# First FFN stage: two gate tiles of a chunk ahead of the next chunk's transposes, and the first chunk rounded and transposed tile by tile

## The reference, cut to what matters

```
x = layernorm(x)                       # 4096 rows of 256
x = act_qdq(x)                         # one scale for the whole tensor: max|x| / 32767, rounded to int16 steps
up   = act_qdq(x @ dequant(w_up).T)    # 256 -> 768
gate = act_qdq(x @ dequant(w_gate).T)  # 256 -> 768, again one scale for the whole tensor
gate = act_qdq(gate * fixed_qdq_u16(sigmoid(gate)))
o    = act_qdq(gate * up)
return o @ dequant(w_down).T
```

## Time and profile before

| | us |
|---|---|
| median of 3 runs | 1246.44 |
| lowest and highest of the 3 | 1245.01, 1251.27 |
| the profiled execution, its own time | 1250.26 |
| its span, first to last instruction | 1248.5 |
| TensorE matmuls busy | 1074.1 (86%) |
| VectorE busy | 954.4 (76%) |
| ScalarE busy | 620.5 (50%) |
| GpSimd busy | 428.0 (34%) |
| mean granted TensorE clock | 0.934 of full speed |

### The profile page before, as it was taken

One profiled execution on the slowest core, in us unless ns is written; L12 is line 12 of the kernel. 1 busy time (PEld: TensorE's weight loads), 2 busy tenths in 40 slices (PEclk: granted clock), 3 DMA queues, 4 the chain that ended last, 5 costly groups with the idle time before them and its releaser, 6 DMA issues. The chain is left out here.

```text
span 1248.5 us, 21557 instructions
## 1 busy us (share of the span) xinstructions
PE 1074.1 (86%) x6208; PEld 897.2 (72%) x6208; DVE 954.4 (76%) x2586; ACT 620.5 (50%) x1332; POOL 428.0 (34%) x514
## 2 busy tenths in 40 slices
PE   7899999995998981039977599999999969999998
PEld 5677777874886760039944588888898858788786
DVE  4798998874675998976554677788878758888886
ACT  1667766761565996977445233333333322333333
POOL 1344444440001882000011235544554443334333
PEclk9999999995998995559999799999999988999999
DMA  8000000000233765702213500101000000000000
GB/s 264 1 2 2 1 1 1 2 1 29 107 120 122 265 252 197 236 22 64 68 43 106 174 1 1 42 0 42 0 0 0 1 1 9 25 18 17 25 17 26
DMA packets 35551, 71.87 MB, mean 58 GB/s; under 512 B 3531, under 2 KB 23071, under 8 KB 35295
## 3 DMA queue, kind: packets, MB, share of 16 engines
q1 hardware_dynamic: 34111, 70.28, 16.9%
q10 hardware_dynamic: 1376, 0.79, 0.3%
HBM read 40.41 MB, written 30.65 MB: 57 GB/s over the span
## 5 line engine op out<-in xcount | busy, mean ns | idle before, releaser
L1068 PE MATMUL a_ps<-VW,a_PT 128*128 (+1 forms) x640 | 143.7, 379 | 0.0
L1068 PEld LDWEIGHTS a_ps<-VW,a_PT 128*128 128x128 f32 x640 | 119.3, 190 | 15.2
L1106 ACT ACTIVATE a_U<-a_U 128x1280 f32<-128x1280 f32 x32 | 40.6, 1270 | 112.6 <-DVE a_U L1179 112.6
L1085 ACT COPY a_PT<-a_ps 128x512 f32<-128x512 f32 (+1 forms) x96 | 46.1, 518 | 90.2 <-PE a_ps L1031 90.2
L1171 DVE TENSOR_REDUCE a_mx<-a_ps 128x4 f32<-128x320 f32 x128 | 62.4, 487 | 33.2 <-PE a_ps L1017 33.0
L1920 PE MATMUL m_ps<-m_wh,m_xh 128*128 128x512 f32 x256 | 87.1, 422 | 0.0
L2018 POOL TENSOR_TENSOR m_half<-m_half 128x512 f32<-128x512 f32 x32 | 41.1, 1283 | 131.9 <-ACT m_half L1980 131.9
L854 DVE TENSOR_SCALAR a_U<-a_ps 128x320 f32<-128x320 f32 x128 | 59.3, 484 | 30.2 <-PE a_ps L662 20.9
L1920 PE MATMUL m_ps<-m_wh,m_xl 128*128 128x512 f32 x256 | 82.0, 402 | 0.0
L1920 PE MATMUL m_ps<-m_wl,m_xh 128*128 128x512 f32 x256 | 81.4, 399 | 0.0
L745 PEld LDWEIGHTS a_ps<-vals,a_PT 128*128 128x128 f32 x640 | 79.7, 199 | 2.2 <-issue 0.4
(11 more groups left out here) (250 smaller groups left out, 3159.2 us busy)
## 6 DMA issues: line engine op xcount, KB each, us to landing
up_scratch<-f_ub SPq DMA_DIRECT2D x24, 512.0 KB, 3.0
f_ul<-up_scratch SPq DMA_DIRECT2D x24, 512.0 KB, 4.5
vw_scratch<-vw_stage SPq DMA_DIRECT2D x8, 640.0 KB, 4.2
VW<-vw_scratch SPq DMA_DIRECT2D x4, 1280.0 KB, 5.8
xs<-in_x SPq DMA_DIRECT2D x4, 1024.0 KB, 12.6
h_scratch<-f_hh SPq DMA_DIRECT2D x8, 512.0 KB, 2.7
h_scratch<-f_hl SPq DMA_DIRECT2D x8, 512.0 KB, 3.2
f_bh<-h_scratch SPq DMA_DIRECT2D x8, 512.0 KB, 4.4
```

Of the source, the lines that this page charges most:

```text
L1068: last = pe.matmul(Y[:, 0:D], PTs[t.p][:, j, :], c["VW"][:].rearrange("p b j d -> p (b j d)")[:, bass.ds(t.batch % 2 * (NJ * D) + j * D, D ...
L1085: act.copy(PTs[t.p][:, js[0]:js[-1] + 1, :].rearrange("p j n -> p (j n)"), R[k][:, 0:len(js) * P]).then_inc(s_PTe, 1)
```

## The change

Three things change, all in the first block.

- TensorE: in step t, gate tiles 0 and 1 of chunk t go first, then the transposes of chunk t+1, then gate tiles 2 to 5. Step -1 holds the transposes of chunk 0 alone. The loops of the transposes are turned round: tile by tile, and both banks of a tile.
- ScalarE and VectorE follow: in step t, the copies and the maxima of gate tiles 0 and 1 of chunk t stand ahead of `hh` and `hl` of chunk t+1.
- Chunk 0 alone is rounded (VectorE), turned back into floats (ScalarE) and transposed (TensorE) tile by tile: four instructions of 128x256 in place of one of 128x1024 on each of the two engines, with a semaphore step after each, and a wait of the transposes for each tile.

```diff
@@ VectorE
                 def body(t):
+                    gate_max(t, range(0, 2))
                     a = t + 1
                     if 0 <= a.t0 < NCH:
...
                             dve.tensor_tensor(hl[a.p][:, k, :], T[k][:], hh[a.p][:, k, :].bitcast(F32),
                                               ALU.subtract).then_inc(s_hl, 1)
-                    gate_max(t, range(0, 2))
                     a = t + 2
...
                         dve.wait_ge(s_hb, a.of(lambda n: n + 1))
-                        dve.tensor_scalar(hq[:], hb[:], ih, None, ALU.mult).then_inc(s_hq, 1)
+                        if a.t0 == 0:
+                            for j in range(TC):
+                                dve.tensor_scalar(hq[:, j, :], hb[:, j, :], ih, None, ALU.mult).then_inc(s_hq, 1)
+                        else:
+                            dve.tensor_scalar(hq[:], hb[:], ih, None, ALU.mult).then_inc(s_hq, 1)
                     gate_max(t, range(2, MF))
@@ TensorE
-                def body(t):
-                    a = t + 1
-                    if 0 <= a.t0 < NCH:
-                        pe.wait_ge(s_hf, a.of(lambda n: n + 1))
-                        if a.t0 >= 1:
-                            pe.wait_ge(s_hl, a.of(lambda n: 2 * n))
-                            pe.wait_ge(s_hh, a.of(lambda n: 2 * n))
+                def transposes(a):
+                    if a.t0 >= NCH:
+                        return
+                    if a.t0 >= 1:
+                        pe.wait_ge(s_hl, a.of(lambda n: 2 * n))
+                        pe.wait_ge(s_hh, a.of(lambda n: 2 * n))
+                    for j in range(TC):
+                        if a.t0 == 0:
+                            pe.wait_ge(s_hf, j + 1)
+                        elif j == 0:
+                            pe.wait_ge(s_hf, a.of(lambda n: n + TC))
                         for k in range(KT):
-                            for j in range(TC):
-                                last = pe.transpose(T[k][:, j * P:(j + 1) * P], hb[:, j, k * P:(k + 1) * P],
-                                                    c["ident"][:])
-                        last.then_inc(s_hT, 1)
-                    if 0 <= t.t0 < NCH:
-                        pe.wait_ge(s_hh, t.of(lambda n: 2 * n + 2))
-                        pe.wait_ge(s_hl, t.of(lambda n: 2 * n + 2))
-                        for m in range(MF):
-                            b = (m + 2 * t.t0) % 4
-                            if m >= 4 or t.t0 >= 1:
-                                pe.wait_ge(s_ev, t.of(lambda n: MF * n + m - 3))
-                            products(pe, R[b][:], 1, m, hh[t.p], hl[t.p]).then_inc(s_mm, 1)
+                            last = pe.transpose(T[k][:, j * P:(j + 1) * P], hb[:, j, k * P:(k + 1) * P],
+                                                c["ident"][:])
+                    last.then_inc(s_hT, 1)
+
+                def gates(t, ms):
+                    for m in ms:
+                        b = (m + 2 * t.t0) % 4
+                        if m >= 4 or t.t0 >= 1:
+                            pe.wait_ge(s_ev, t.of(lambda n: MF * n + m - 3))
+                        products(pe, R[b][:], 1, m, hh[t.p], hl[t.p]).then_inc(s_mm, 1)
+
+                def body(t):
+                    if t.t0 < 0:
+                        transposes(t + 1)
+                        return
+                    pe.wait_ge(s_hh, t.of(lambda n: 2 * n + 2))
+                    pe.wait_ge(s_hl, t.of(lambda n: 2 * n + 2))
+                    gates(t, range(0, 2))
+                    transposes(t + 1)
+                    gates(t, range(2, MF))
@@ ScalarE
                 def body(t):
+                    gate_out(t, range(0, 2))
                     a = t + 1
...
                             act.copy(hh[a.p][:, k, :], T[k][:]).then_inc(s_hh, 1)
-                    gate_out(t, range(0, 4))
+                    gate_out(t, range(2, 4))
                     a = t + 2
                     if 0 <= a.t0 < NCH:
-                        act.wait_ge(s_hq, a.of(lambda n: n + 1))
-                        act.copy(hb[:], hq[:]).then_inc(s_hf, 1)
+                        if a.t0 == 0:
+                            for j in range(TC):
+                                act.wait_ge(s_hq, j + 1)
+                                act.copy(hb[:, j, :], hq[:, j, :]).then_inc(s_hf, 1)
+                        else:
+                            act.wait_ge(s_hq, a.of(lambda n: n + TC))
+                            act.copy(hb[:], hq[:]).then_inc(s_hf, 1)
                     gate_out(t, range(4, MF))
```

More of the change, by code:

```diff
@@ L1615, in _ @@
                 spread_max(pe, 0)
-                def body(t):
-                    a = t + 1
-                    if 0 <= a.t0 < NCH:
-                        pe.wait_ge(s_hf, a.of(lambda n: n + 1))
-                        if a.t0 >= 1:
-                            pe.wait_ge(s_hl, a.of(lambda n: 2 * n))
-                            pe.wait_ge(s_hh, a.of(lambda n: 2 * n))
-                        for k in range(KT):
-                            for j in range(TC):
-                                last = pe.transpose(T[k][:, j * P:(j + 1) * P], hb[:, j, k * P:(k + 1) * P],
-                                                    c["ident"][:])
-                        last.then_inc(s_hT, 1)
-                    if 0 <= t.t0 < NCH:
-                        pe.wait_ge(s_hh, t.of(lambda n: 2 * n + 2))
-                        pe.wait_ge(s_hl, t.of(lambda n: 2 * n + 2))
-                        for m in range(MF):
-                            b = (m + 2 * t.t0) % 4
-                            if m >= 4 or t.t0 >= 1:
-                                pe.wait_ge(s_ev, t.of(lambda n: MF * n + m - 3))
-                            products(pe, R[b][:], 1, m, hh[t.p], hl[t.p]).then_inc(s_mm, 1)
@@ new lines, in transposes @@
+                def transposes(a):
[9 more added lines that the diff above has]
+                            pe.wait_ge(s_hf, a.of(lambda n: n + TC))
+                        for k in range(KT):
+                            last = pe.transpose(T[k][:, j * P:(j + 1) * P], hb[:, j, k * P:(k + 1) * P],
+                                                c["ident"][:])
+                    last.then_inc(s_hT, 1)
```

## The result

The changed kernel takes 1242.74 us (median of 22 runs, 1241.01 to 1245.89). The kernel before took 1246.63 us beside it (22 runs, 1241.84 to 1252.01). The ratio is 0.9968, with a 95% interval of 0.9958 to 0.9977: 3.9 us faster, clear of the noise and under the 0.5% that was called a measurable change. The forecast was 1242.1 us. The profiled execution took 1243.19 us with a span of 1241.5 us, 7.1 us less than that of the profiled execution before (1248.5), which took 3.8 us more than the median of its runs.

A forecast was written before the change was run, and what follows sets the result against it. Steady chunks were taken as bound by TensorE's work, the first block's start by waits in TensorE's order. 1250.26 - 4.3 = 1245.96 us profiled, the same difference off the median 1246.44 giving 1242.1; range 1238.8 to 1246.5.

The forecast's parts named there:

- The order as the fault: First block's start: chunk 0's gate tiles, ready at 309.91 us, queue behind chunk 1's transposes, which wait to 313.06 us.
- The split: Chunk 0 tile by tile: first transposes at 304.87 for 306.00, `hl` at 308.78 for 309.91; 1.13 us saved, bounds 0 to 1.25.
- The gate tiles ahead: First block's start: third gate tile at 314.05 us in place of 318.35, 4.3 us earlier, clock rising after 3.2 us.
- The steady chunks: First block's later chunks: everything hidden, costed at nothing; `hl` has 3.6 us to spare, the floats 3.2 us.
- From the block to the total: Whole program: the block's 4.3 us come off the profiled 1250.26 us, and the same difference off the median 1246.44.
- The rival of the later blocks: Second block's clock may rise after 3.2, not 6.2 us: another 1.5 us, again at a further start; 1239.1 us, chance 0.12.
- One sign of being wrong: Whole profiled execution: the forecast is wrong if the span is less by more than 6 us.
- The other signs: First transposes near 304.9, `hl` near 308.8, chunks of 9.24 us, chunk 1's transposes not waiting, second block's matmuls near 387.7.

The follow-up runs named there:

- the five tiles ahead: Changed kernel with five gate tiles in place of two ahead of the next chunk's transposes; 1254.17 us, ratio 1.0061 to the kernel before.
- the warm start: Changed kernel with nine extra unread matmuls on TensorE around chunk 0's transposes, five before and four behind; 1243.93 us, again 1243.07 us.
- the end fill: Changed kernel with eleven extra unread matmuls on TensorE at the first block's end, while it waits for the gate's scale; 1241.71 us, ratio 0.9967.
- the gate tiles alone: Changed kernel without chunk 0's tile by tile treatment, only two gate tiles moved ahead; 1245.64 us (ratio 0.9992), again 1245.85 us (0.9994).
- the delay: Changed kernel with two unread VectorE instructions of 128x256 ahead of the gate's scale at the first block's end; 1241.97 us.

## Why the prediction was right

**The order as the fault, right.** TensorE waited at the first chunk for chunk 1's floats with the gate tiles ready (no matmul ran from 309.91 to 313.12 us), and the edit removed that wait. The experiments bear out each edit by itself within the block.

**The split, right in size at the start of the chain.** 1.13 us were forecast, 1.04 measured. The first tile was rounded in 0.39 us including the handover (301.96 to 302.35), where I had 0.34. ScalarE's casts took 0.40 us each and 1.32 us together. I had taken 0.376 from a neighbouring shape, 0.02 too little. As worked out, it didn't matter: TensorE's eight transposes still took 1.97 us. Over the block the split brought about half of this, 0.4 to 0.55 us. The sum let the clock's rise move with TensorE's start, and the experiments show it where it was, or nearly so (12.27 us after the first rounding against 12.23).

**The gate tiles ahead, right with one term mis-sized.** The handover from `hl` to TensorE took 0.15 us, not 0.04, and the clock rose 4.2 us after the first gate matmul, not 3.2. That made 3.76 us at the third gate tile in place of 4.3, inside the bounds of 2.8 to 5.5. Another 0.1 us went in the steady part (3.65 at the last gate matmul).

**The steady chunks, right.** 9.24 us before and after, and no wait. The slacks were 0.3 us too generous, as the five tiles ahead showed; the first loads for the second block were issued up to 372.79 us and took 6.5 us at most, well ahead of 386.26.

**From the block to the total, right in the number and wrong in the reason.** I took it that a gain in the block reaches the total whole: "the ramp is in every run, so I take the same difference from the median". That the cold stretches behind the block differ from run to run and cancel was my assumption, and no row showed it. The profiles show the length of the second block's cold stretch go with the place of its first matmul behind the fall of the clock: the clock rises 3.2 to 3.4 us after a first matmul that comes 0.1 to 0.2 us behind the fall, and 6.0 to 6.2 us after one that comes 0.6 to 0.8 us behind it. Both single edits and the warm start speak against the assumption: 3.2 us won in the block came out as 0.3, 0.5 as 0.0, and 5.6 as 2.0 and 3.1. The rival of the later blocks was there, with 1.5 us for each and "Nothing in the trace speaks for it over the opposite". It is real. In the profiles it made 0.9 to 1.1 us at the second block, where 1.5 were said, and 1.8 up to L1068, of which 1.4 came back after it. The medians say that it goes one way more often in one kernel than in another. For the changed kernel it comes to almost nothing: 3.65 us in the block, 3.7 to 3.9 in the total. That the forecast of 4.3 us came so near is in part luck, then: the same sum would have missed for either edit alone by 2.5 and 1.1 us, and for the warm start by 2.5 to 3.6.

**One sign of being wrong came true.** I had written that I am wrong if the span is less by more than 6 us, and it is 7.1 us less. Of this 2.15 us lie ahead of the first rounding, 3.65 in the block, 0.9 in *next*, 1.8 in *behind*, and 1.5 were lost after L1068. The sign was badly chosen: two single executions of a kernel can lie further apart than that, as the three runs before the change did with 6.3 us. The other signs, which count from the block, came out as forecast.

What stays open is why a kernel leans to one side, and how firmly it does. It is argued, not shown, that the rise in the first block fixes a moment from which a set amount of work leads to the second block's start, so that this start falls at much the same place against the clock in most runs. In eight of the eleven profiles without the end fill it is 75.1 us from that rise to the fall ahead of the second block, and in these eight the second block's first matmul comes 0.1 to 0.8 us behind the fall; the two warm starts have 78.5 us there and the five tiles ahead 81.9. The runs themselves carry only the mean clock of the whole program. How the 3.4 us between the changed kernel and the gate tiles alone divide over the program is known from single profiles only, and these show 0.5 us in the block and 1.4 behind it; the rest lay ahead of the block, in code that is the same.

## What to carry to other kernels

Where an engine's program is written by hand, look in the ramp of each stage for work that is ready behind an instruction that waits; two tiles moved ahead, with the first chunk split, won 3.7 us in the stage here, and cost nothing at two tiles; at five, the moved work made `hl` late and cost 1.1 us per chunk. Measure such an edit by the stage's own milestones in the profile as well as by the total: a total can hide 3 us won in a stage, or show more than was won. A profile's milestones depend on where the clock rose (the block here was 74.95 to 74.97 us plus half the time to the rise), so compare them at the same place of the rise. And where TensorE waits for some microseconds between two dense stages (4.80 us here), matmuls with no use in that gap can keep the half clock out of the next stage: the granted clock was 1.00 at the second block's start with them and 0.50 without. 20 of them together with the new order won 7.0 us here. The later starts they left cold: from 673.9 to 690.9 us the granted clock was 0.50 in the profile of the end fill, 17.1 us where the changed kernel had 13.7. And the runs with the end fill are spread over 5.6 and 5.4 us, no less than the changed kernel's 4.5 and the gate tiles' 5.0 without.

## What was not expected of the hardware

The same second block, which starts 84 us after the first rounding, took 81.0, 82.5 or 83.5 us from the last gate matmul on, depending on whether the clock stayed up, rose 3.2 to 3.4 us after its first matmul, or 6.0 to 6.2 us after. The last two go with some 0.5 us in the place of that first matmul: 0.1 to 0.2 us after the fall of the clock against 0.6 to 0.8 us. This is seen in nine profiles, and in one of them, the delay, it was brought about by an edit.

In the first block, starting TensorE's work 1.04 us earlier saved 0.55 us, because the clock's rise stayed at its place and did not move with the start: 12.27 us after the first rounding against 12.23, and with two gate tiles ahead 8.80 to 8.86 us without the split against 8.51 to 9.12 with it.

A TensorE instruction that waits for VectorE's `hl` started 0.14 to 0.15 us after it in the ramp, at half clock (changed kernel) and at full clock (warm starts) alike, and 0.24 us after it in the chunks of the five tiles ahead. Both are several times the 0.04 us after which ScalarE started behind VectorE here (304.86 to 304.90).
